# Starting the second mixture of experts inside linear attention, quantizing its successor's weights later, and three new orders around slot attention

## The chip, the cores and the metric

One core of one Trainium2 chip runs the whole network in a single launch. The metric is the device time in microseconds (us); the kernel before was run three times: 758.55, 759.08 and 763.17 us, median 759.08. Five engines work at the same time, each through its own list of instructions in order: TensorE (PE, matrix products into the accumulator memory PSUM), VectorE (DVE), ScalarE (ACT), GpSimd (POOL) and the queue SP that issues transfers. They are tied together by semaphores alone: an instruction waits until a counter has reached a number. Everything is 32-bit floating point.

## The reference, cut to what matters

The input is x, 8 batches of 512 tokens of 128 features. Six stages follow each other, each added to x (the layer norms have no weights):

```
x = x + 0.5 * MoE(layernorm(x))          # moe_a
x = x + LinearAttention(layernorm(x))    # linatt: causal, 16 heads of 8
x = x + 0.5 * MoE(layernorm(x))          # moe_b, same weights as moe_a
x = x + 0.5 * FFN(layernorm(x))          # ffn_a: fp4-quantized SwiGLU
x = x + SlotAttention(layernorm(x))      # att: softmax over the 8 batches, per token
x = x + 0.5 * FFN(layernorm(x))          # ffn_b, same weights as ffn_a

MoE: logits = xn @ router_w.T; top 2 of 8 experts, softmax over the two;
     expert: square(relu(xn @ w1[e])) @ w2[e]
FFN: q(xn) @ q(w_gate).T, q(xn) @ q(w_up).T; h = silu(gate) * up; q(h) @ q(w_down).T
q:   per block of 16: scale = max|.| / 6, round to {0, .5, 1, 1.5, 2, 3, 4, 6}, times scale
```

## The kernel before, in words

The program is one hand-written function. Inside it each engine has one list; per stage there is a function on each engine (`moe`, `linatt`, `ffn`, `att`), and the stages are called one after the other. The order of the calls in the code is the order on the engine; no planner exists. The whole x stays in on-chip memory (`x_sb`). A dictionary `S[stage]` holds the semaphores; `body(i, ...)` is the work of batch (or group, or slot) `i`, and early bodies stand in hardware loops (`Fori`).

**Mixture of experts.** For each of 8 batches (512 tokens) and 8 experts: TensorE makes `up(i, e)` (512 columns) into bank 2 or 3, ScalarE takes ReLU (L595) and then the square (L599), TensorE makes `down(i, e)` from the square (four products of 128x128) into one of the four banks 4 to 7, and VectorE adds it to x with the gate as factor (`accumulate`, L1070, four instructions). `down` waits until the bank was emptied four experts earlier (`out_free`). The gates come from `router` (TensorE), `gating` (VectorE, L1028 to L1047, ended by the ranks), an exponential `gate_exp` on ScalarE after expert 2 (L590), and `gating_end` (VectorE, L1051 to L1055). The layer norm of a later batch is statistics on VectorE (`ln_stats`, L985, L994), four small operations on GpSimd (`ln_group` or `layer_norm`), `normalise` on ScalarE (L577), `transposes` on TensorE and a copy back (`evac_xnT`, L584).

**Linear attention**, per batch: products, scores and states on TensorE; masks and the picking of head parts on VectorE (`scores` L1145, `pick` L1154 to L1165, `residual` L1173); `within` and `across` are the products inside and across chunks, in two halves; `project_out` is the last one. In its last batch only those steps are left. The weights of the feed-forward network lie in `fraw` (128x1152), and the object `w4` quantizes them on VectorE in these steps: `largest` L916, `scales` L922 and L924, `inverse` L935, `divide` L943, a magnitude on ScalarE (L533), `snap` L949, `unbias` L954, `rescale` L960. Before, the first five stand in the last batch of linear attention and the rest around the first gating of moe_b.

**Feed-forward**, per group of 512 tokens: quantize the normalised rows (`x_scales` on VectorE, `x_divide` on GpSimd, `x_squares` and `x_offsets` on ScalarE, `x_snap` on VectorE L1017, `x_back` on GpSimd L450 and L453, `x_transposes` on TensorE L1441, `evac_xnT`), four `gate_up(g, j)` (TensorE) with a `silu` each (ScalarE, L723), the product with the up-projection on VectorE (L1346; it opens the group), the quantization of the hidden values, transposes and `down`.

**Slot attention**, four slots of 1024 rows: VectorE makes query-key products (`qk`, L1239, eight), TensorE sums them per head (`score`), ScalarE copies (`scores_half`, L761), TensorE turns them (`turn`, L1710), VectorE subtracts the maximum (`less_max`, L1247), ScalarE takes exponentials, VectorE normalises and multiplies with the values (`pv`, L1267, eight), GpSimd adds pairs (`slot_pairs`, L408), TensorE sums (`context`, eight) and projects (`project_out`), ScalarE writes x (`x_out`, L773). The last slot also starts ffn_b.

## Time and profile before

| | us |
|---|---|
| median of three runs | 759.08 |
| the profiled execution, its own time | 757.82 |
| its span from first to last instruction | 756.0 |
| TensorE busy | 673.3 |
| VectorE busy | 606.9 |
| ScalarE busy | 458.5 |
| GpSimd busy | 294.7 |

Busy times overlap, so they do not add up to the span. A matmul's end is modelled in the profile. TensorE's granted clock over the whole span was 0.959 of full speed.

### The profile page before, as it was taken

What the parts mean: (1) busy time and instruction counts of PE and PEld (TensorE: products, weight loads), DVE (VectorE), ACT (ScalarE), POOL (GpSimd) and SP (SyncE); (2) the same over time, 40 slices, a digit from 0 to 9 for tenths busy, and PEclk for the clock granted to TensorE, in tenths of its full rate; (3) what the DMA queues carried; (4) which work ended last, traced back from release to release, by engine and by line L of the source; (5) the groups of instructions that cost most, each with busy time, mean ns of one, the idle gap of its engine ahead of it and who ended that gap; (6) DMA issues with size and microseconds to landing.
All of it is one profiled execution on the core that took longest, in us unless ns stands there. A gap on an engine that the chain in (4) does not pass through costs nothing.

```text
span 756.0 us, 16397 instructions
## 1 busy us (share of the span) xinstructions
PE 673.3 (89%) x5826; PEld 481.9 (64%) x5826; DVE 606.9 (80%) x1554; ACT 458.5 (61%) x867; POOL 294.7 (39%) x417
## 2 busy tenths in 40 slices
PE   4999999789999879999997789898978987799996
PEld 2777776567888757777764456565646556456664
DVE  2788787846766678887786999999999997899983
ACT  3787788674674328777786476757454433666642
POOL 5000120156556310011013677554534527668520
PEclk9999999879999989999999799999999998899996
DMA  8000000000000000000000000000000000000000
GB/s 207 22 0 0 0 1 1 0 3 4 2 0 3 4 1 1 0 0 0 0 1 2 0 1 0 1 2 0 3 0 0 0 0 1 0 29 15 24 19 29
DMA packets 13461, 7.08 MB, mean 9 GB/s; under 512 B 1177, under 2 KB 13409, under 8 KB 13409
## 3 DMA queue, kind: packets, MB, share of 16 engines
q1 hardware_dynamic: 11328, 5.33, 2.6%
q10 hardware_dynamic: 2080, 1.05, 0.5%
q8 instruction: 33, 0.54, 0.3%
q14 instruction: 20, 0.16, 0.1%
HBM read 4.28 MB, written 2.10 MB: 8 GB/s over the span
## 4 chain that ended last, share of the span: by engine, by line
PE 61%; DVE 18%; ACT 10%; issue 7%; POOL 3%; DMA 1%; DVEq 0%; POOLq 0%; ACTq 0%
PE ps L1427 56%; DVE shared L1267 4%; DVE shared L1239 3%; PE ps L1778 2%; DVE x_sb L1070 2%; ACT ffn_work L533 2%; ACT ffn_work L723 2%; PE ps L1435 1%; DVE stats L985 1%; ACT xnT L584 1%; ACT x_sb L832 1%; PE ps L1441 1%; ACT ffn_work L571 1%; ACT hqT L828 1%; DVE ps L1259 1%
## 5 line engine op out<-in xcount | busy, mean ns | idle before, releaser
L1427 PEld LDWEIGHTS ps<-w_sb,sq_h 128*128 128x128 f32 x1024 | 132.3, 193 | 70.6 <-ACT sq_h L599 51.8
L1070 DVE SCALAR_TENSOR_TENSOR x_sb<-ps,gates,x_sb 128x128 f32 (+1 forms) x512 | 147.2, 344 | 24.2 <-PE ps L1427 20.3
L1427 PE MATMUL ps<-w_sb,sq_h 128*128 128x128 f32 x1024 | 138.5, 279 | 1.8 <-ACT sq_h L599 1.8
L1427 PE MATMUL ps<-xnT,w_sb 128*128 128x512 f32 x256 | 135.7, 614 | 0.0
L353 POOL TENSOR_SCALAR vareps<-meanvar 128x4 f32<-128x4 f32 (+1 forms) x28 | 8.9, 319 | 265.7 <-DVE meanvar L994 265.3
L595 ACT ACTIVATE relu_h<-ps 128x512 f32<-128x512 f32 x128 | 75.6, 591 | 56.5 <-PE ps L1427 56.2
L599 ACT ACTIVATE sq_h<-relu_h 128x512 f32<-128x512 f32 x128 | 80.6, 630 | 4.0
L1427 PE MATMUL ps<-gateT,xnT 128*128 128x352 f32 x128 | 58.9, 544 | 14.7 <-ACT ffn_work L723 13.0
L577 ACT ACTIVATE xn<-x_sb,shift,rstd 128x128 f32 (+1 forms) x136 | 57.0, 481 | 10.1 <-POOL shift L361 8.3
L400 POOL TENSOR_TENSOR shared<-shared 128x128 f32<-128x128 f32 x112 | 51.0, 455 | 27.7 <-ACT shared L678 19.5
L1427 PE MATMUL ps<-downT,hqT 128*128 128x128 f32 x384 | 57.5, 289 | 4.2 <-ACT hqT L828 3.9
L1427 PEld LDWEIGHTS ps<-downT,hqT 128*128 128x128 f32 x384 | 49.4, 197 | 10.7 <-ACT hqT L828 10.4
L723 ACT ACTIVATE ffn_work<-ps 128x352 f32<-128x352 f32 x64 | 29.5, 461 | 40.3 <-PE ps L1427 40.2
L1427 PE MATMUL ps<-upT,xnT 128*128 128x352 f32 x128 | 51.5, 486 | 0.0
L828 ACT ACTIVATE hqT<-ps 128x384 f32<-128x384 f32 x64 | 29.6, 487 | 32.3 <-PE ps L1778 31.5
L408 POOL TENSOR_TENSOR shared<-shared 128x512 f32<-128x512 f32 x32 | 43.2, 1378 | 13.2 <-DVE shared L1267 13.2
L1427 PEld LDWEIGHTS ps<-gateT,xnT 128*128 128x128 f32 x128 | 21.3, 203 | 42.2 <-ACT ffn_work L723 33.3
L1239 DVE TENSOR_TENSOR shared<-shared 128x1024 f32<-128x1024 f32 x32 | 42.2, 1386 | 0.1
L1427 PEld LDWEIGHTS ps<-xnT,w_sb 128*128 128x128 f32 x256 | 40.1, 197 | 2.1 <-issue 2.1
L438 POOL TENSOR_TENSOR ffn_work<-xn,fq_x_r 128x512 f32<-128x512 f32 x16 | 16.9, 1057 | 59.3 <-DVE fq_x_r L939 59.3
L1427 PE MATMUL ps<-ident,shared 128*128 128x128 f32 x256 | 33.7, 287 | 6.1 <-POOL shared L408 6.0
L1346 DVE TENSOR_TENSOR ffn_work<-ffn_work,ps 128x1408 f32<-128x1408 f32 x16 | 25.9, 1619 | 15.9 <-PE ps L1427 15.9
(166 smaller groups left out, 1355.9 us busy)
## 6 DMA issues: line engine op xcount, KB each, us to landing
x_sb<-in_L_attn_x_dram SPq DMA_DIRECT2D x8, 256.0 KB, 7.5
out_dram<-x_sb SPq DMA_DIRECT2D x8, 256.0 KB, 2.3
w_sb<-in_L_ffn_w_all_dram ACTq DMA_DIRECT2D x2, 512.0 KB, 6.5
wraw<-in_L_attn_qkv_w_dram SPq DMA_DIRECT2D x1, 192.0 KB, 4.4
wraw<-attn_in_proj_weight_dram SPq DMA_DIRECT2D x1, 192.0 KB, 3.3
fraw<-in_L_ffn_w_down_dram SPq DMA_DIRECT2D x1, 176.0 KB, 3.1
fraw<-in_L_ffn_w_gate_dram SPq DMA_DIRECT2D x1, 128.0 KB, 2.7
fraw<-in_L_ffn_w_up_dram SPq DMA_DIRECT2D x1, 128.0 KB, 2.4
```

The source lines that it names most:

```text
L400: nc.gpsimd.tensor_tensor(st[:, k, :], st[:, k, :], st[:, k - 1, :], ALU.add).then_inc(s["prefix_ready"], 1)
L408: nc.gpsimd.tensor_tensor(prod[:, b, 0:B // 2, :], prod[:, b, 0:B // 2, :], prod[:, b, B // 2:B, :], ALU.add).then_inc(s["pair_ready"], 1)
L577: a = nc.scalar.activation(xn[:, into + j, :], tile(i, j), ACT.Identity, scale=rstd[:, j:j + 1], bias=shift[:, j:j + 1])
L595: nc.scalar.activation(relu_h[:, e % 2, :], bank(2 + e % 2, T), ACT.Relu).then_inc(s["relu_done"], 1)
L599: nc.scalar.activation(sq_h[:, e % 2, :], relu_h[:, e % 2, :], ACT.Square).then_inc(s["sq_ready"], 1)
L723: nc.scalar.activation(silu_g[:, j, :], bank(k, FI), ACT.Silu).then_inc(s["silu_ready"], 1)
L828: nc.scalar.activation(hqT[:, j % 2, :, :], bank(6 * (1 - j % 2), 3, P), ACT.Copy).then_inc(s["hT_ready"], 1)
L1070: t = nc.vector.scalar_tensor_tensor(tile_b(i, j), bank(4 + e % 4, TPB, C)[:, j, :], gates[:, j, e:e + 1], tile_b(i, j), ALU.mult, ALU.add)
L1239: nc.vector.tensor_tensor(prod[:, b, :, :], kT[:, :, :], qT[:, b, :].unsqueeze(1).to_broadcast([P, B, P]), ALU.mult).then_inc(s["qk_ready" ...
L1267: nc.vector.tensor_tensor(prod[:, b, :, :].rearrange("p a (h d) -> p a h d", h=H), v_att[:, :, :].rearrange("p a (h d) -> p a h d", h=H), ...
L1346: nc.vector.tensor_tensor(h3.rearrange("p (j k) w -> p j k w", k=KB), silu_g[:, :, :].rearrange("p j (k w) -> p j k w", w=BLK), ps[:, 2:6, ...
L1427: return nc.tensor.matmul(o, a, b, start=start, stop=stop, **kw)
```

## The change

Five things are changed, and no arithmetic is.

1. **moe_b begins inside the last batch of linear attention.** TensorE issues `router(0, 0)`, `up(0, 0)`, `up(0, 1)` and `down(0, 0)` between the steps of that batch; the first router writes bank 0 instead of bank 1 (`router_bank`). VectorE does `gating(0)` and `gating_end(0)` there, where the weights' quantization stood. The wait for all of linear attention (`x_done`) stands before the router of batch 1 now. Batches 0 and 1 are written out in front of the loops.
2. **The weights' quantization is spread**: `largest` and `scales` stay in linear attention (later in the batch), `inverse`, `divide` follow expert 1 of moe_b's batch 0, `snap` its expert 6, `unbias` and `rescale` experts 1 and 4 of batch 1. The magnitude on ScalarE follows expert 5 of batch 0.
3. **The last two batches of moe_b**: the statistics for ffn_a's first group stand after expert 4 of batch 6, not after expert 5.
4. **Slot attention's first half score** of a slot is issued at the end of the previous slot; that of slot 0 in the last group of ffn_a, in front of `down(7, 2)`, and its `turn` in front of the wait for ffn_a's results.
5. **Last slot and start of ffn_b**: `x_snap(0)` and `x_back(0)` earlier; `x_transposes` and `gate_up(0, 0)` after the second context, `gate_up(0, 1)` to `gate_up(0, 3)` in a row after the first `project_out`, and the last four contexts behind them.

```diff
@@ ScalarE, moe
-                        if e == 2:
+                        if e == 2 and (first or type(i) is not int or i > 0):
                             gate_exp(i)
+                        if e == 5 and not first and type(i) is int and i == 0:
+                            act.wait_ge(s_fv, 1)
+                            magnitude(fq_h[0][:, 0:6 * P + FK], fq_h[1][:, 0:6 * P + FK]).then_inc(s_fm, 1)
@@ ScalarE, last slot
                     exp_half(i, 1)
+                    evac_xnT(nxt, 0, k=2)
                     normal(nxt, False, 1)
+                    silu(nxt, 0, 0, 3)
                     ctx_half(i, 0)
                     x_out(i, 0)
-                    evac_xnT(nxt, 0, k=2)
-                    for j in range(TPB):
+                    for j in range(1, TPB):
                         silu(nxt, 0, j, 6)
-                    ctx_half(i, 1)
                     x_squares(nxt, 1)
                     x_offsets(nxt, 1)
+                    ctx_half(i, 1)
                     x_out(i, 1)
@@ VectorE, moe
-                        if e == 5 and more:
+                        if more and e == (5 if ahead or first else 4):
...
+                        if not first and type(i) is int and i < 2:
+                            if (i, e) == (0, 1):
+                                w4.inverse()
+                                w4.divide()
+                            if (i, e) == (0, 6):
+                                w4.snap()
+                            if (i, e) == (1, 1):
+                                w4.unbias()
+                            if (i, e) == (1, 4):
+                                w4.rescale()
@@ VectorE, last batch of linear attention
                     if not more:
-                        dve.wait_ge(s_fw, 80)
-                        w4.largest()
-                        w4.scales()
-                        w4.inverse()
+                        gating(0, lambda j: None)
                     pick(i, 0, side)
...
                     if not more:
-                        w4.divide()
+                        gating_end(0)
+                        dve.wait_ge(s_fw, 80)
+                        w4.largest()
+                        w4.scales()
                     pick(i, 1, side)
@@ VectorE, last slot
                     pv(i, 1)
+                    if not more:
+                        x_snap(nxt, 0)
                     less_max(i, 1)
...
                     pv(i, 3)
-                    if not more:
-                        x_snap(nxt, 0)
@@ TensorE, moe
+                    if not first and type(i) is int and i == 1:
+                        pe.wait_ge(S["linatt"]["x_done"], GROUPS)
...
-                    pe.wait_ge(s["out_free"], i * E + e + 1)
+                    if first or type(i) is not int or i > 0 or e >= 4:
+                        pe.wait_ge(s["out_free"], i * E + e + 1)
@@ TensorE, last slot
                     for b in range(4):
                         context(i, b)
+                        if not more and b == 1:
+                            pe.wait_ge(front.s["lin_ready"], 6 * TPB)
+                            x_transposes(nxt, 0, 2)
+                            gate_up(nxt, 0, 0, 3)
                     project_out(i, 0)
                     if not more:
-                        pe.wait_ge(front.s["lin_ready"], 6 * TPB)
-                        x_transposes(nxt, 0, 2)
+                        for j in range(1, TPB):
+                            if j > 1:
+                                pe.wait_ge(s["pv_ready"], B * i + 4 * (j - 1))
+                            gate_up(nxt, 0, j, 6)
                     for b in range(4, B):
                         context(i, b)
-                        if not more:
-                            if b >= 6:
-                                pe.wait_ge(s["pv_ready"], B * i + 4 * (b - 5))
-                            gate_up(nxt, 0, b - 4, 6)
                     project_out(i, 1)
+                    if more:
+                        front.score(i + 1, 0)
+                        front.turn(i + 1, 0)
@@ TensorE, ffn
                     hidden_transposes(g, 3)
+                    if first and g == GROUPS - 1:
+                        pe.wait_ge(s["hT_ready"], g * TPB + 3)
+                        front.score(0, 0)
                     down(g, 2)
```

On TensorE, in the last batch of linear attention and at the start of moe_b (`rT` is the router, `w1_sb` an up, `w2_sb` a down product, `wT,attT` a `project_out`, `shared` alone an `across`, `shared,v_tok` a `within`), the list before was:

```order
L1427 MATMUL ps<-shared,v_tok 32x128 x32
L1427 MATMUL ps<-shared 128x128 x7
L1427 MATMUL ps<-wT,attT 128x128 x4
L1427 MATMUL ps<-shared,v_tok 32x128 x32
L1427 MATMUL ps<-shared 128x128 x8
L1427 MATMUL ps<-wT,attT 128x128 x4
L1427 MATMUL ps<-rT,xnT 128x8 x4
L1427 MATMUL ps<-xnT,w1_sb 128x512
```

and now it is:

```order
L1453 MATMUL ps<-rT,xnT 128x8 x4
L1453 MATMUL ps<-shared,v_tok 32x128 x32
L1453 MATMUL ps<-shared 128x128 x7
L1453 MATMUL ps<-wT,attT 128x128 x4
L1453 MATMUL ps<-xnT,w1_sb 128x512
L1453 MATMUL ps<-shared,v_tok 32x128 x32
L1453 MATMUL ps<-shared 128x128 x8
L1453 MATMUL ps<-xnT,w1_sb 128x512
L1453 MATMUL ps<-w2_sb,sq_h 128x128 x4
L1453 MATMUL ps<-wT,attT 128x128 x4
```

The router, two up products and one down product now stand between the steps of linear attention.

On VectorE at the same place (`picked` and `attT` are a `pick`, `fq_h_max` is `largest`, the first row the last mask) the list before was:

```order
L1145 TENSOR_TENSOR shared<-ps,causal 128x512 x2
L916 TENSOR_REDUCE fq_h_max<-fraw 128x72
L922 TENSOR_SCALAR fq_h_s<-fq_h_max 128x72
L924 TENSOR_SCALAR fq_h_r<-fq_h_max 128x72
L935 RECIPROCAL fq_h_r<-fq_h_r 128x72
L1154 TENSOR_SCALAR picked<-ps,headsel 128x256
...
L1173 TENSOR_TENSOR x_sb<-ps,x_sb 128x512
L943 TENSOR_TENSOR ffn_work<-fraw,fq_h_r 128x1152
L1154 TENSOR_SCALAR picked<-ps,headsel 128x256
```

and now it is:

```order
L1170 TENSOR_TENSOR shared<-ps,causal 128x512 x2
L1038 COPY logits<-ps 128x32
L1041 TENSOR_REDUCE top<-logits 128x4
...
L1057 TENSOR_REDUCE rank<-diff 128x32
L1179 TENSOR_SCALAR picked<-ps,headsel 128x256
...
L1198 TENSOR_TENSOR x_sb<-ps,x_sb 128x512
L1061 SCALAR_TENSOR_TENSOR ex<-rank,exs 128x32
...
L926 TENSOR_REDUCE fq_h_max<-fraw 128x72
...
L1179 TENSOR_SCALAR picked<-ps,headsel 128x256
```

The gating took the place of the first four steps on the weights, and `gating_end`, `largest` and `scales` that of `divide`.

On TensorE in the last slot (`ident,shared` is a `context`, `wT,turned` a `project_out`, `ident,xn` the transposes for ffn_b, `gateT` and `upT` a `gate_up`) the list before was:

```order
L1427 MATMUL ps<-ident,shared 128x128 x16
L1427 MATMUL ps<-wT,turned 128x128 x4
L1441 MATMUL ps<-ident,xn 128x128 x4
L1427 MATMUL ps<-ident,shared 128x128 x4
L1427 MATMUL ps<-gateT,xnT 128x352
L1427 MATMUL ps<-upT,xnT 128x352
L1427 MATMUL ps<-ident,shared 128x128 x4
```

and now it is:

```order
L1453 MATMUL ps<-ident,shared 128x128 x8
L1467 MATMUL ps<-ident,xn 128x128 x4
L1453 MATMUL ps<-gateT,xnT 128x352
L1453 MATMUL ps<-upT,xnT 128x352
L1453 MATMUL ps<-ident,shared 128x128 x8
L1453 MATMUL ps<-wT,turned 128x128 x4
L1453 MATMUL ps<-gateT,xnT 128x352
L1453 MATMUL ps<-upT,xnT 128x352
```

Before, four pairs of `context` and `gate_up` followed the transposes; now one `gate_up` stands between the contexts, three follow `project_out` in a row, and four contexts (x16) come behind them.

## Rows read from the trace of the kernel before

**Rows 1.** The page: busy time, share and instructions of each engine; chain that ended last.

```profile
PE 673.3 (89%) x5826; PEld 481.9 (64%) x5826; DVE 606.9 (80%) x1554; ACT 458.5 (61%) x867; POOL 294.7 (39%) x417
...
PE 61%; DVE 18%; ACT 10%; issue 7%; POOL 3%; DMA 1%; DVEq 0%; POOLq 0%; ACTq 0%
```

**Rows 2.** Timeline, 261 to 284 us: start, us, engine, line, operation, [idle before <-releaser].

```profile
261.04 1.15 PE L1427 MATMUL ps<-shared,v_tok 32*32 32x128 f32 x64 [2.46 <-DVE shared L1145]
...
266.29 1.14 PE L1427 MATMUL ps<-shared,v_tok 32*32 32x128 f32 x64 [1.46 <-DVE attT L1165]
...
268.04 1.16 ACT L533 ACTIVATE ffn_work<-ffn_work 128x1152 f32<-128x1152 f32 x1 [15.01 <-DVE ffn_work L943]
...
271.67 1.16 PE L1427 MATMUL ps<-wT,attT 128*128 128x128 f32 x8 [2.26 <-DVE attT L1165]
...
275.11 1.36 DVE L954 SCALAR_TENSOR_TENSOR ffn_work<-ffn_work 128x1152 f32<-128x1152 f32 x1
...
281.39 1.05 PE L1427 MATMUL ps<-w_sb,sq_h 128*128 128x128 f32 x8
...
283.00 0.19 DVE L1051 SCALAR_TENSOR_TENSOR ex<-rank,exs 128x32 f32<-128x32 f32 x1 [2.93 <-ACT exs L590]
```

**Rows 3.** Windows: busy us of each engine, then TensorE's granted clock (PEclk).

```profile
276.00:280.00 4.00, 4.00 (x10) 1.93 (x9) 3.83 (x12) 2.05 (x4) 0.00 (x0) 0.50 0.00 0
...
630.00:640.00 10.00, 9.22 (x49) 8.09 (x49) 7.36 (x15) 3.98 (x6) 8.73 (x10) 0.73 0.01 2
```

**Rows 4.** Timeline, gating between batches 1 and 2 of moe_b.

```profile
310.12 0.35 DVE L1070 SCALAR_TENSOR_TENSOR x_sb<-ps,gates,x_sb 128x128 f32 x1 [1.15 <-PE ps L1427]
...
311.28 0.18 DVE L1038 TENSOR_TENSOR ex<-logits,top 128x32 f32<-128x32 f32 x1
...
313.81 0.21 ACT L590 ACTIVATE exs<-ex 128x32 f32<-128x32 f32 x1
```

**Rows 5.** Timeline, from batch 6 to batch 7 of moe_b.

```profile
388.01 0.88 ACT L577 ACTIVATE xn<-x_sb,shift,rstd 128x128 f32<-128x128 f32 x2 [1.80 <-POOL shift L429]
...
390.08 1.16 PE L1427 MATMUL ps<-w_sb,sq_h 128*128 128x128 f32 x8 [0.78 <-ACT sq_h L599]
...
393.55 0.19 DVE L1051 SCALAR_TENSOR_TENSOR ex<-rank,exs 128x32 f32<-128x32 f32 x1 [1.01 <-ACT exs L590]
```

**Rows 6.** Timeline, from ffn_a to the first slot.

```profile
517.36 10.37 DVE L1239 TENSOR_TENSOR shared<-shared 128x1024 f32<-128x1024 f32 x8
...
526.49 1.92 PE L1427 MATMUL ps<-shared,headcols 128*32 128x512 f32 x16 [1.26 <-ACT x_sb L832]
...
529.82 0.69 DVE L1247 TENSOR_REDUCE red<-ps 128x64 f32<-128x512 f32 x1 [2.09 <-PE ps L1710]
```

**Rows 7.** Timeline, last slot and the start of ffn_b.

```profile
621.19 0.69 DVE L1247 TENSOR_REDUCE red<-ps 128x64 f32<-128x512 f32 x1
...
625.92 1.65 DVE L1017 TENSOR_TENSOR ffn_work<-ffn_work 128x512 f32<-128x512 f32 x1
...
630.00 1.06 POOL L453 TENSOR_TENSOR xn<-ffn_work,fq_x_s 128x512 f32<-128x512 f32 x1
...
631.59 2.08 PE L1427 MATMUL ps<-wT,turned 128*128 128x128 f32 x8 [0.78 <-ACT turned L767]
...
635.73 0.76 PE L1427 MATMUL ps<-gateT,xnT 128*128 128x352 f32 x2
...
637.81 0.76 PE L1427 MATMUL ps<-gateT,xnT 128*128 128x352 f32 x2
...
643.35 1.62 DVE L1346 TENSOR_TENSOR ffn_work<-ffn_work,ps 128x1408 f32<-128x1408 f32 x1 [5.81 <-PE ps L1427]
...
645.13 0.60 ACT L773 ACTIVATE x_sb<-ps 128x512 f32<-128x512 f32 x1
...
649.79 1.51 PE L1427 MATMUL ps<-gateT,xnT 128*128 128x352 f32 x2 [0.73 <-issue]
...
658.03 1.62 DVE L1346 TENSOR_TENSOR ffn_work<-ffn_work,ps 128x1408 f32<-128x1408 f32 x1 [1.09 <-PE ps L1427]
```

More of the change, by code:

```diff
@@ L1128, in linatt @@
+                return gating, gating_end, run
+            def linatt(s, nxt, follow):
+                gating, gating_end, _ = follow
                 ch = Chain(dve, s["dve_chain"])
```

180 lines of the change are left out of this document (99 added, 81 removed).

## The prediction

> **What bounds the kernel now.** I read the page first, then the chain of waits and the timeline at the four places that the change touches. TensorE is busy for 89% of the span, VectorE for 80%; 61% of the chain that ended last is TensorE's, 18% VectorE's [rows 1]. So no one engine bounds the whole: the mixtures of experts run at TensorE's pace, slot attention and the feed-forward groups mostly at VectorE's. What the change can give lies where one stage hands over to the next, and there the rows show gaps. At the end of linear attention TensorE waits three times, 2.46, 1.46 and 2.26 us, each time for VectorE [rows 2]. Then moe_b starts from nothing: the second `down` product begins at 281.39, 9.7 us after the last `project_out` (271.67), and VectorE waits 2.93 us for the first exponential. From 276 to 280 TensorE's granted clock is 0.50, the 1.2 GHz level [rows 3]. Around batch 7 of moe_b ScalarE waits 1.80 us for a layer norm's shift [rows 5]. At the first slot VectorE waits 2.09 us [rows 6]; at ffn_b's start 5.81 us, and 1.09 us before its second group [rows 7]. These gaps together are the most that reordering can take out.
>
> **Part 1: moe_b begins early.** The router needs only batch 0's normalised rows, which were copied back long before; it goes in front of the `within` that begins at 261.04, inside a wait of 2.46 us. `up(0, 0)` goes in front of the one at 266.29, inside 1.46 us. `up(0, 1)` and `down(0, 0)`, about 1.8 us, go behind the last `across`, inside the 2.26 us before 271.67 [rows 2]. All four are hidden, and `project_out` keeps its place. VectorE's gating (some 2.3 us, as were the four steps on the weights that stood there) ends before `pick` can start. `gating_end`, `largest` and `scales` (about 2.6 us) replace `divide`, and fit in the 1.4 us of `divide` and the 1.5 us that VectorE waited there, with 0.1 us to spare. Up to 271.67 nothing moves. After it, `project_out` runs to 272.8, `up(0, 2)` takes 0.9, and `down(0, 1)` begins at about 273.6 in place of 281.39: **7.8 us** gained. Its square is ready, since ScalarE had nothing else to do.
>
> Against that: the magnitude (1.16 us, rows 2) used to run while ScalarE waited 15.01 us, and now stands behind expert 5, between squares for which TensorE waits. It costs between 0 (if the transposes cover it) and 1.16 us. I take 0.6, since transposes follow that expert. VectorE gets `inverse`, `divide`, `snap` (3.3 us) in batch 0 and `unbias`, `rescale` (2.7 us, two of 1.36, rows 2) in batch 1. The cover in batch 0 is that it begins to accumulate at once after the last residual: there is no wait of 2.93 us any more, and it has about 16 us for 17 us of work from a start that is earlier than TensorE needs. In batch 1 the 2.7 us make the next gating late. VectorE waits 1.15 us before that gating now, so 1.6 us remain; the difference that `gate_exp` needs is ready at 311.46 and used at 313.81 [rows 4], 2.35 us later. So 0.75 us of cover is left, and the banks that `down` needs come free over 2 us early. If the cover goes, what is late next is the exponential, and behind it on ScalarE every ReLU. I set this at 0. Part 1 is 7.8 - 0.6 = **7.2 us**. Bounds: 7.8 with the magnitude hidden; 3.8 if the clock falls to 1.2 GHz all the same for the 7 us that such a stretch lasts here (half of 7 is 3.4).
>
> **Part 2: statistics one expert earlier.** VectorE does them while it would wait for expert 5, so the shift that ScalarE waits for at 388.01 comes about 1.2 us earlier, of the 1.80 us. TensorE's wait of 0.78 us before 390.08 goes, and the exponential comes earlier, for which VectorE waits 1.01 us before 393.55; what VectorE does before it (`x_scales`) does not move [rows 5]. From there to ffn_a VectorE is busy with accumulations, so the end moves with it: **0.9 us**, between 0 and 1.0.
>
> **Part 3: half score 0 in ffn_a.** VectorE's fourth product ends half way through the eight that began at 517.36, at 522.6; the score (1.92 us) can run at 523.7, before two `down` products. Those, and the last `x_out` of ffn_a, are delayed by these 1.9 us, from 526.25 (the end of the wait before 526.49) to 528.2. The `turn` is done by then. `less_max` waits for that result too and starts at 528.2 in place of 529.82 [rows 6]: **1.6 us**, between 0 (if a table load falls between the copy and the exponential) and 2.1 (VectorE's whole wait). Queued behind the added wait on TensorE are only these `down` products. In the other slots the same instructions follow in the same sequence, and VectorE has no gap to give: 0.
>
> **Part 4: last slot and ffn_b.** `x_snap` moves from 625.92 to where `less_max` starts now, 621.19. The transposes wait for `x_back`, which ended at 631.06; 4.7 us earlier, and without a pair of GpSimd's in front of it, is 625.4. The pairs for contexts 2 and 3 now come behind `x_back` and a layer norm on GpSimd, and end at about 630, so `project_out` stays where it is (631.59). From its end three steps of `gate_up` and `silu` remain. A step with a context in it takes 2.08 us (635.73 to 637.81), without it between 1.2 (its own matmuls) and 2.08; I take 1.4, nearer to the matmuls. So the first group of ffn_b can start at about 637.5 to 638, which is also when VectorE is free (643.35 - 5.81 = 637.5): 5.6 us earlier [rows 7].
>
> Not all of it lasts. The four contexts that were mixed in now follow in a row (3.7 us), so the second `project_out` and its `x_out`, at 645.13 now, come only 1.5 to 2 us earlier. Behind that `x_out` on ScalarE stand the third layer norm and the copy for which `gate_up(1, 0)` at 649.79 waits. ScalarE no longer waits for GpSimd's `x_back(1)` between them, as that is early too, which gives 1.7 us more: `gate_up(1, 0)` at about 646.1. With the clock as now, the second group (658.03) moves by the same 3.7 us; from there the groups follow at their old distance. I take **3.7 us**. Upper end 5.3: the clock stays at 2.4 GHz here, and VectorE's own chain is the limit. Lower end 1.2: the clock falls before the first group as now (0.73 over 630 to 640, rows 3), and the contexts behind it are late.
>
> `x_snap` takes 1.65 us at 625.92, while GpSimd works on pairs. The Trainium skill ("SBUF — State Buffer", section "Who interferes with whom") says that a VectorE operation with two inputs in SBUF and a GpSimd operation that reads SBUF exclude each other, and the later one waits for the whole of the first. By that rule the new place, beside GpSimd's second pair, buys nothing in duration and the sum stays as below; without it the sum could grow by a part of these 1.65 us. I leave the duration at 1.65.
>
> **The sum.** 7.2 + 0.9 + 1.6 + 3.7 = 13.4 us. The profiled execution took 757.82 (span 756.0), so it would take 744.4. It lies 1.3 us under the median of the runs shown; from the median, 759.08 - 13.4 = **745.7 us**, which I name.
>
> **Rivals.**
> - *The clock falls in the last slot all the same.* For it: even now a fall lies there, and the new order still leaves gaps before the `gate_up`s. Against it: the longest gap, from the second context to the transposes, gets shorter and is filled by transposes and a `gate_up`. Part 4 then gives 1.2: 748.2 us. The Trainium skill ("TensorE: Matmul & The Clock Gate", section "A second HAM failure mode: psum-queue depth-cycling") says that short idle times between groups of matmuls can make the clock swing; it speaks for this rival. Chance 0.2.
> - *The clock falls at moe_b's start.* TensorE is denser from 261 to 273 than now, when it did fall [rows 2, 3]. Gain 3.4 less: 749.1 us. Chance 0.08.
> - *Slower: VectorE never catches up.* Place: gating in moe_b from batch 1 on. If each of the six later batches starts late by the 2.7 us of `unbias` and `rescale`, because TensorE's waits move along with VectorE and leave it no slack, that is 16.2 us lost against 13.4 gained: 761.9 us. It decides when the lateness passes the 2.35 us of cover [rows 4] and VectorE's waits are gone. Against it stands that VectorE waits 1.15 us in each batch now. Chance 0.03.
> - *The early start isn't early*: something that I take for ready (the exponential, the bank, `x_done`) holds moe_b back, and Part 1 shrinks to under 2 us: 751 us or more. Nothing in the rows speaks for it. Chance 0.07.
> - The forecast itself, 743 to 747: 0.57. The rest is a better case (both clocks high): 742.9.
>
> **How the numbers follow.** All upper ends: 7.8 + 1.0 + 2.1 + 5.3 = 16.2, so 742.9 from the median and 741.6 from the profiled execution. The low end is 741.5. The high end takes in both clock rivals together (745.7 + 2.5 + 3.4 = 751.6): 752. About 0.15 is left out. One per cent, 7.6 us, is what can be told from no change: under 751.5 is faster. Only the slower rival and part of the fourth lie above: faster 0.89, same 0.08, slower 0.03.
>
> **What would show it.** In the new profile: the router and `down(0, 0)` before the last `project_out`, and `down(0, 1)` at about 273.6; a granted clock of 1.00 from 273 to 281; no ScalarE wait before the normalise after batch 6; `less_max` 1.6 us earlier in its stage; the first group of ffn_b 5.6 us and the second 3.7 us earlier in their stage. Wrong would be: TensorE waiting for squares in batch 1 of moe_b, the exponential late, or a wait of some microseconds in front of the transposes in the last slot.

## The result and the profile after

| | before | after |
|---|---|---|
| first comparison, median (us) | 759.06 (4 runs, 758.55 to 763.17) | 740.63 (4 runs, 740.18 to 744.41) |
| all executions of this study, median | 758.58 (66 runs) | 741.27 (13 runs) |
| profiled execution, its own time | 757.82 | 744.41 |
| its span | 756.0 | 742.5 |
| granted clock over the span | 0.959 | 0.970 |

The ratio of the first comparison is 0.9759 (95% interval 0.9723 to 0.9796); of a second one, in five rounds, 0.9791 (0.9762 to 0.9821). The kernel is faster by 17 to 18 us where 13.4 were forecast: 740.63 lies 5.1 us under the 745.7 named, and just under the low end, 741.5. Between the two profiled executions the difference is 13.4 us, by chance the forecast to a tenth; two more profiled executions of the changed kernel took 742.32 and 741.70.

The page of the profile after, against [rows 1]:

```profile
PE 667.8 (90%) x5826; PEld 478.1 (64%) x5826; DVE 605.7 (82%) x1554; ACT 458.4 (62%) x867; POOL 295.1 (40%) x417
...
PE 64%; DVE 15%; ACT 10%; issue 6%; POOL 3%; DMA 1%; DVEq 0%; POOLq 0%; ACTq 0%
```

The same instructions, and the same busy times but for 5.5 us of TensorE and 1.2 of VectorE: waits and slow clock were taken out, not work, and the chain now runs through VectorE for 15% in place of 18%.

The timeline of the profile after, from linear attention's last batch to batch 2 of moe_b, against [rows 2, 4] (the lines of the code moved: L1453 was L1427, L536 L533, L593 L590, L1061 L1051):

```profile
260.07 1.06 PE L1453 MATMUL ps<-rT,xnT 128*128 128x8 f32 x8
...
262.60 1.96 PE L1453 MATMUL ps<-shared,v_tok 32*32 32x128 f32 x64 [1.48 <-DVE shared L1170]
...
267.96 0.48 DVE L1179 TENSOR_SCALAR picked<-ps,headsel 128x256 f32<-128x256 f32 x1 [3.31 <-PE ps L1453]
...
275.66 1.16 PE L1453 MATMUL ps<-wT,attT 128*128 128x128 f32 x8 [0.51 <-DVE attT L1190]
...
277.52 1.05 PE L1453 MATMUL ps<-w_sb,sq_h 128*128 128x128 f32 x8
...
284.46 1.15 ACT L536 ACTIVATE ffn_work<-ffn_work 128x1152 f32<-128x1152 f32 x1
...
294.42 0.21 ACT L593 ACTIVATE exs<-ex 128x32 f32<-128x32 f32 x1
...
309.95 0.21 ACT L593 ACTIVATE exs<-ex 128x32 f32<-128x32 f32 x1
...
310.28 0.19 DVE L1061 SCALAR_TENSOR_TENSOR ex<-rank,exs 128x32 f32<-128x32 f32 x1 [0.22 <-ACT exs L593]
```

The router fills a part of the wait (1.48 us remain of 2.46). `project_out` waits 0.51 us in place of 2.26, and the second `down` follows it after 1.86 us instead of 9.7. But the `within` at 262.60 took 1.96 us, not 1.15: the clock fell there, and VectorE waited 3.31 us. (The size of a clock fall is given below as what is missing to full clock: a stretch of 6.8 us at 0.50 is a fall of 3.4 us.) Windows of the same profile (granted clock third from the end):

```profile
262.00:270.00 8.00, 7.40 (x88) 6.48 (x88) 4.45 (x16) 0.23 (x1) 0.00 (x0) 0.57 0.01 3
273.00:281.00 8.00, 7.49 (x44) 5.40 (x43) 7.22 (x26) 3.95 (x7) 1.70 (x4) 1.00 0.00 0
628.00:636.00 8.00, 6.69 (x49) 5.76 (x48) 6.97 (x12) 3.20 (x7) 4.93 (x7) 1.00 0.01 2
636.00:640.00 4.00, 2.09 (x4) 1.18 (x4) 2.46 (x12) 3.54 (x7) 1.06 (x1) 0.72 0.00 0
```

The fall at 273 to 281 [rows 3] is gone, but one stands at 262 to 270. In the last slot the one over 630 to 640 is gone too, and a short one begins behind 637.

The rest of the timeline after, against [rows 5 to 7]: normalise and exponential of batch 7; half score and first maximum of slot 0; rounding step, GpSimd's pair, second maximum, and ffn_b's first two groups:

```profile
382.80 0.88 ACT L580 ACTIVATE xn<-x_sb,shift,rstd 128x128 f32<-128x128 f32 x2 [0.44 <-POOL shift L433]
...
388.41 0.21 ACT L593 ACTIVATE exs<-ex 128x32 f32<-128x32 f32 x1
...
517.74 1.92 PE L1453 MATMUL ps<-shared,headcols 128*32 128x512 f32 x16
...
522.07 0.69 DVE L1272 TENSOR_REDUCE red<-ps 128x64 f32<-128x512 f32 x1 [0.23 <-ACT x_sb L840]
...
613.45 0.85 DVE L1027 TENSOR_TENSOR ffn_work<-ffn_work 128x512 f32<-128x512 f32 x1
613.71 1.72 POOL L412 TENSOR_TENSOR shared<-shared 128x512 f32<-128x512 f32 x1
...
614.23 0.68 DVE L1272 TENSOR_REDUCE red<-ps 128x64 f32<-128x512 f32 x1
...
629.61 1.62 DVE L1371 TENSOR_TENSOR ffn_work<-ffn_work,ps 128x1408 f32<-128x1408 f32 x1 [0.78 <-PE ps L1453]
...
637.91 1.51 PE L1453 MATMUL ps<-gateT,xnT 128*128 128x352 f32 x2 [2.39 <-issue]
...
645.20 1.62 DVE L1371 TENSOR_TENSOR ffn_work<-ffn_work,ps 128x1408 f32<-128x1408 f32 x1 [0.37 <-PE ps L1453]
```

VectorE's waits of 2.09 us at slot 0, 5.81 and 1.09 us at ffn_b are down to 0.23, 0.78 and 0.37.

**Stage by stage.** A dozen instructions that occur in every version cut the span into stages: exponentials of moe_a (batch 7) and moe_b (batches 1, 6, 7), the product with the up-projection of ffn groups 0 and 1 (and 7), the maxima of the slots. Each number is the difference of two starts in a trace. The stages that are left out (batches 1 to 6 of moe_b, 77.96; groups 1 to 7, 75.86 to 75.90; slots 0 to 3, 84.57 to 84.83) differ in these eleven profiles by 0.26 us at most.

| profile | start to moe_a | linear attention, moe_b begins | batch 6 to 7 | to ffn_a group 1 | to slot 0 | slot 3 to ffn_b group 1 | end | span |
|---|---|---|---|---|---|---|---|---|
| before | 130.37 | 167.91 | 17.07 | 36.15 | 24.49 | 43.61 | 22.10 | 756.0 |
| before_look | 130.15 | 167.61 | 17.06 | 36.13 | 24.49 | 43.61 | 22.10 | 755.4 |
| after | 131.58 | 162.84 | 16.02 | 35.13 | 22.64 | 38.51 | 21.36 | 742.5 |
| after_again | 130.55 | 161.27 | 16.03 | 35.27 | 22.62 | 38.33 | 22.02 | 740.4 |
| after_look | 130.42 | 160.73 | 16.03 | 35.21 | 22.63 | 38.41 | 22.03 | 739.7 |
| part1_only | 130.47 | 163.08 | 17.06 | 35.92 | 24.49 | 42.46 | 22.14 | 750.2 |
| part2_only | 131.33 | 171.94 | 16.02 | 35.36 | 24.49 | 42.24 | 22.08 | 757.8 |
| part3_only | 130.73 | 168.73 | 17.06 | 35.76 | 22.62 | 42.03 | 22.02 | 753.3 |
| part4_only | 130.65 | 168.98 | 17.07 | 35.93 | 24.49 | 39.24 | 22.11 | 753.0 |
| snap_early_only | 130.20 | 168.13 | 17.06 | 35.76 | 24.50 | 43.70 | 22.03 | 755.7 |
| snap_late | 129.79 | 161.96 | 16.02 | 35.14 | 22.63 | 43.66 | 22.05 | 745.5 |

### The profile page after: what moved, and what is told of

It is laid out like the page before. It is cut to its first block, busy times and chain, and to the rows that moved or that the text cites. A ratio compares the mean times of both kernels' runs of the same rounds, so it can differ in the third digit from the quotient of the medians.

```text
span 742.5 us, 16304 instructions
## 1 busy us (share of the span) xinstructions
PE 667.8 (90%) x5826; PEld 478.1 (64%) x5826; DVE 605.7 (82%) x1554; ACT 458.4 (62%) x867; POOL 295.1 (40%) x417
## 3 DMA queue, kind: packets, MB, share of 16 engines
q10 hardware_dynamic: 2080, 1.05, 0.5%
## 4 chain that ended last, share of the span: by engine, by line
PE 64%; DVE 15%; ACT 10%; issue 6%; POOL 3%; DMA 1%; DVEq 0%; POOLq 0%; ACTq 0%
PE ps L1453 59%; DVE shared L1292 3%; DVE shared L1264 3%; PE ps L1826 2%; ACT ffn_work L731 2%; DVE x_sb L1081 2%; ACT ffn_work L536 2%; PE ps L1461 2%; ACT ffn_work L574 1%; ACT xnT L587 1%; ACT x_sb L840 1%; DVE stats L995 1%; PE ps L1467 1%; ACT ffn_work L569 1%; ACT hqT L836 1%
## 5 line engine op out<-in xcount | busy, mean ns | idle before, releaser
L1453 PEld LDWEIGHTS ps<-w_sb,sq_h 128*128 128x128 f32 x1024 | 132.1, 192 | 69.6 <-ACT sq_h L602 50.3
L1453 PE MATMUL ps<-w_sb,sq_h 128*128 128x128 f32 x1024 | 138.2, 278 | 1.4 <-ACT sq_h L602 1.3
L1453 PE MATMUL ps<-xnT,w_sb 128*128 128x512 f32 x256 | 134.3, 607 | 0.0
L1453 PE MATMUL ps<-gateT,xnT 128*128 128x352 f32 x128 | 57.4, 532 | 17.6 <-ACT ffn_work L731 13.4
L1453 PE MATMUL ps<-downT,hqT 128*128 128x128 f32 x384 | 57.0, 286 | 4.2 <-ACT hqT L836 4.0
L1453 PEld LDWEIGHTS ps<-downT,hqT 128*128 128x128 f32 x384 | 48.7, 195 | 11.6 <-ACT hqT L836 10.4
L1453 PEld LDWEIGHTS ps<-gateT,xnT 128*128 128x128 f32 x128 | 20.5, 198 | 46.4 <-ACT ffn_work L731 34.0
L1453 PE MATMUL ps<-upT,xnT 128*128 128x352 f32 x128 | 50.2, 475 | 0.0
L412 POOL TENSOR_TENSOR shared<-shared 128x512 f32<-128x512 f32 x32 | 43.3, 1380 | 13.1 <-DVE shared L1292 13.1
L1453 PEld LDWEIGHTS ps<-xnT,w_sb 128*128 128x128 f32 x256 | 39.7, 195 | 1.0 <-issue 1.0
L995 DVE BATCH_NORM_STATS2 stats<-x_sb 128x6 f32 (+1 forms) x144 | 30.7, 279 | 9.0 <-DMA x_sb<-in_L_attn_x_dram 5.1
L1292 DVE TENSOR_TENSOR shared<-shared,ps 128x1024 f32<-128x1024 f32 x32 | 37.2, 1215 | 0.6 <-DVE ps L1284 0.4
```

The lines of the kernel that those rows point to most:

```text
L412: nc.gpsimd.tensor_tensor(prod[:, b, 0:B // 2, :], prod[:, b, 0:B // 2, :], prod[:, b, B // 2:B, :], ALU.add).then_inc(s["pair_ready"], 1)
L995: ch.add(nc.vector.bn_stats(stats[:, j, :], tile(i, j)))
L1292: nc.vector.tensor_tensor(prod[:, b, :, :].rearrange("p a (h d) -> p a h d", h=H), v_att[:, :, :].rearrange("p a (h d) -> p a h d", h=H), ...
L1453: return nc.tensor.matmul(o, a, b, start=start, stop=stop, **kw)
```

## The experiments

Numbers after "measured" are the median, and the ratio to before with its 95% interval.

**The four parts alone.** Each is the kernel before with the lines of one part of the change and nothing else: part 4 (last slot and ffn_b), part 3 (half scores), part 1 (moe_b begun early, quantization spread), part 2 (one line). The lines are those of the diff further up:

```diff
-                        if e == 5 and more:
+                        if more and e == (5 if ahead or first else 4):
```

> Only the last slot and the start of ffn_b are in the new order. The prediction's size for it was 3.7 us (755.4). The trace of the change says more: between the last slots and ffn_b's second group it gained 5.1 us, and 0.7 at the end; by that theory this kernel takes 753.3, with the first group of ffn_b some 6 us and the second 5 us earlier in their stage, and one clock fall of 3.4 us less in 628 to 656. If the gain there needs the half score of part 3, it stays at 3.7 or under.

Measured: 755.05; 0.9944 (0.9922 to 0.9967). That is 3.5 us, by the median the prediction's 3.7 and not the 5.1 of the theory. In the profile the stage took 39.24 in place of 43.61, with the first group 5.3 and the second 4.4 us earlier, and one fall of 1.7 us stands in the last slot (629 to 632). That the gain needs part 3 is not so: further down the stage takes 38.86 without it.

> Only the half scores are moved: that of slot 0 into the last group of ffn_a, those of the other slots to the end of the slot before. The prediction said 1.6 us for slot 0 and 0 for the other slots (757.5); the trace of the change shows 1.85 at slot 0 (757.2). A rival: in the last slot, whose rest stays in the old order, the early score shifts TensorE's idle time and the clock, and the gain is 0 or 3.4 more.

Measured: 755.14; 0.9964 (0.9948 to 0.998). Slot 0's stage is 1.87 us shorter, as in the changed kernel; the other slots nothing. The last stage took 42.03 in place of 43.61. That is not the half score: part1_only and part2_only, which touch nothing there, took 42.46 and 42.24. In all three the first clock fall of the last slot is of 1.7 us, in before of 3.4. How long this stage takes in the old order depends on that fall.

> Only moe_b is begun early and the weights' quantization spread. The prediction said 7.2 us (751.9). Theory A: part 1 is worth 8 to 9 us where TensorE's clock does not fall inside linear attention's last batch, since the transition gains 7.8 and a clock fall less there gives more, so 750.5; the 5.1 us of the profiled execution of the change was a fall at 262 to 269. Theory B: that fall is there in most executions, and part 1 gives 5.1 us (754.0).

Measured: 749.76; 0.9881 (0.9862 to 0.99). Theory A by the timing (8.8 us, six executions), theory B by the stage (4.8 us, one execution, 163.08 for 167.91), as this profile has a fall of 3.4 us at 261 to 268.

> Only the statistics for ffn_a's first group are moved from expert 5 to expert 4 in moe_b's batch 6. The prediction said 0.9 us (758.2). The trace of the change shows 1.05 us at the exponential of batch 7, and 1.05 more before ffn_a's second group, where a VectorE wait for up-products shrinks from 1.00 to 0.37; if that belongs to this part, it is worth 2.1 us (757.0).

Measured: 758.51; 0.9994 (0.9975 to 1.0012). The two stages of this part are 1.05 and 0.4 to 0.8 us shorter in the profile, the median is not: its linear attention, which the change does not touch, took 171.94 with falls at 261 to 269 and 275 to 286. A microsecond of true gain drowns in that. Of part 2 only the stage is shown, not the time.

**Is the profiled execution typical?**

> The changed kernel once more, unaltered, for a second profiled execution. The first one's own time was 744.41, 3.8 above the median of its runs, with a fall of TensorE's clock at 262 to 270, inside linear attention's last batch. Theory A: in a usual execution that fall is absent or shorter, batch 1's exponential of moe_b stands some 3 us earlier than 294.42, and the median is 740.6. Theory B: the fall is there too, and the 3.8 us come from elsewhere (ffn_a's start, ffn_b, the beginning).

> The kernel before once more, for a second profiled execution. The first is 1.2 us under the median. Theory A: it was lucky at the end of linear attention (one clock fall, at 273 to 281, where four other profiles with the old order there have two), so from moe_a's last exponential to moe_b's second one this one takes 168.5 to 170 in place of 167.91. Theory B: that stage is the same and the difference lies in the last slot or the beginning.

> The changed kernel once more, a third profiled execution. Stage by stage the two profiles so far give 162.84 and 161.27 for linear attention and the start of moe_b. Theory A: the typical value is 161.3 to 162, the clock falls in linear attention's last batch in about half of the executions, and part 1 is worth 7 to 7.8 us. Theory B: it is nearer 160.5, and part 1 is worth the 8.8 us that it gained when timed alone.

Measured: after_again 741.58, 0.9791 (0.9762 to 0.9821); one execution each of the other two, 757.26 and 741.70. For before, neither theory: the second profile repeats the first in all stages within 0.3 us, and is 0.7 under the median of its comparison (757.98) again. For after, the first profile was the untypical one; the third has no fall in linear attention's last batch and takes 160.73 there, near the 160.5 of theory B. Windows of after_again:

```profile
262.00:270.00 8.00, 6.98 (x163) 5.82 (x164) 6.65 (x22) 1.46 (x3) 0.00 (x0) 1.00 0.02 5
...
273.00:281.00 8.00, 7.94 (x48) 5.92 (x49) 7.45 (x26) 5.30 (x11) 1.69 (x4) 1.00 0.00 0
```

and its timeline:

```profile
262.34 1.14 PE L1453 MATMUL ps<-shared,v_tok 32*32 32x128 f32 x64 [1.48 <-DVE shared L1170]
...
273.06 1.16 PE L1453 MATMUL ps<-wT,attT 128*128 128x128 f32 x8 [0.51 <-DVE attT L1190]
...
274.92 1.05 PE L1453 MATMUL ps<-w_sb,sq_h 128*128 128x128 f32 x8
...
291.82 0.21 ACT L593 ACTIVATE exs<-ex 128x32 f32<-128x32 f32 x1
```

No fall. From the last `within` to the second `down` it is 12.58 us, against 20.35 before [rows 2]: 7.77 us, where 7.8 were forecast. To batch 1's exponential it is 29.48, against 37.24 (261.04 to 298.28): 7.76, so the magnitude cost nothing on the way.

**Filling the wait in linear attention.** The changed kernel and behind the first router:

```diff
                         router(0, 0)
+                        pe.wait_ge(s["x_done"], GROUPS - 2)
+                        for _ in range(3):
+                            mm(bank(1, T), w1_sb[:, 0, :], xnT[:, 0:T])
                     within(i, 0, side)
```

> The changed kernel with three more products of 512 columns behind the first router, into bank 1, which nothing reads before it is overwritten; they fill TensorE's wait of 1.48 us before the last batch's within product. Theory A, the fall at 262 to 270 is set off by that wait: the granted clock stays at 1.00 there, and the median falls by up to 3 us, to 738 to 740. Theory B, it comes from the denser or sparser stretch before and is only moved: the same time within 1 us, a fall of 3.4 us elsewhere between 255 and 290. If the fillers are longer than the wait, up to 0.3 us is lost.

Measured: 742.44; 0.9793 (0.9767 to 0.9819). The three products took 2.82 us, more than the wait of 1.48 that they were to fill:

```profile
260.31 2.82 PE L1453 MATMUL ps<-xnT,w_sb 128*128 128x512 f32 x6
...
263.06 1.15 PE L1453 MATMUL ps<-shared,v_tok 32*32 32x128 f32 x64
```

No fall followed, but the time did not change. It tells little: after_again has none either, without a filler, and the filler is longer than the gap (the `within` begins 132.6 us after moe_a's last exponential, 131.8 in after_again). What sets the fall off stays open.

**Does VectorE catch up?** The changed kernel with the last step on the weights three times:

```diff
-                                w4.rescale()
+                                w4.rescale(2)
@@ def rescale(self, extra=0)
+                    for _ in range(extra):
+                        self.ch.need(self.ch.add(nc.vector.tensor_tensor(self.dst3, blocks(self.v), self.wide(self.sl), ALU.mult)))
```

> The changed kernel with the rescaling of the weights done three times instead of once, in batch 1 of moe_b after expert 4: 2.7 us more for VectorE just before the gating of batch 2. In the trace of the change that gating's end waited 0.22 us for the exponential. The prediction's slower rival said that a lateness there repeats in each of the six later batches (up to 15 us more). The forecast said that it is a single delay, caught up through VectorE's waits of about 1.15 us a batch: exp(2) up to 2.5 us later, and 0 to 2.5 us in all.

Measured: 746.28; 0.9845 (0.9816 to 0.9875). Its exponential of batch 2 waited for VectorE:

```profile
302.14 2.74 DVE L971 TENSOR_TENSOR fraw<-ffn_work,fq_h_s 128x1152 f32<-128x1152 f32 x2
...
310.98 0.23 ACT L593 ACTIVATE exs<-ex 128x32 f32<-128x32 f32 x1 [1.45 <-DVE ex L1050]
```

Of 2.72 us added (two operations of 1.36), 1.55 were lost at batch 2 (exponential to exponential 17.08 in place of 15.53) and 1.2 covered. The four later batches together lost 0.05. It is a single delay, and the rival's mechanism is refuted. The rest of the 5.0 us over 741.27 goes in part with TensorE's clock. Linear attention's stage is 2.1 us longer than in after_again, with a fall of 3.4 us at 261 to 268 that the latter has not. Another at 609 to 616 cost nothing that its stage shows (38.41).

**The magnitude elsewhere.** The changed kernel with

```diff
-                        if e == 5 and not first and type(i) is int and i == 0:
+                        if e == 3 and not first and type(i) is int and i == 0:
```

> The changed kernel with the magnitude on ScalarE behind expert 3 of moe_b's batch 0, where a half of a layer norm's rows follows it (0.86 us) and no transposes, in place of behind expert 5. The prediction set its cost behind expert 5 at 0.6 us because transposes cover it; the traces show 0 there (from the second down product to batch 1's exponential 16.90 us, 16.89 before). If the transposes are the cover, down products are late by up to 1.16 us here and stay so; if ScalarE's free half microsecond per expert is the cover, nothing is lost (within 0.3 us) by batch 1's exponential.

Measured: 746.0; 0.982 (0.9801 to 0.9839).

```profile
281.37 1.16 ACT L536 ACTIVATE ffn_work<-ffn_work 128x1152 f32<-128x1152 f32 x1 [1.34 <-DVE ffn_work L953]
...
284.50 0.84 PE L1453 MATMUL ps<-w_sb,sq_h 128*128 128x128 f32 x4 [2.26 <-ACT sq_h L602]
```

More than either theory said: ScalarE waits 1.34 us for VectorE's `divide`, then spends 1.16, TensorE waits 2.26 us, and a clock fall of 1.7 us follows. From the second `down` (276.82) to the exponential (297.72) it is 20.90 in place of 16.90. An operation that is free at expert 5 costs 4 at expert 3. The input's readiness decides, which neither theory had named; which of the two covers it is at expert 5 was not separated.

**The halves of part 4.** The changed kernel with VectorE's `x_snap` in its old place (snap_late), and the kernel before with only `x_snap` on VectorE and `x_back` on GpSimd early (snap_early_only):

```diff
@@ snap_late, VectorE, last slot
-                    if not more:
-                        x_snap(nxt, 0)
                     less_max(i, 1)
...
                     pv(i, 3)
+                    if not more:
+                        x_snap(nxt, 0)
```

> The changed kernel with VectorE's rounding step for ffn_b's first group back in its old place, after the fourth value product of the last slot; TensorE's and ScalarE's new order stays. If the early rounding is what part 4 lives on, ffn_b's first group starts 4 to 5 us later relative to its slot (22.92 us after the slot's first maximum now) and the second 3 us later, so the kernel takes about 743.5; if TensorE's order is what counts, the loss is under 1 us. The rounding took 0.85 us in the new place and 1.65 in the old one; here it should take 1.65 again.

> The kernel before with one half of part 4 alone: VectorE's rounding step and GpSimd's step back for ffn_b's first group early, the order of TensorE and ScalarE as before. With the other half alone (the kernel with the late rounding) the second group of ffn_b stood 43.7 us after the third slot's maximum, with both 38.5, in the old order 42.0 to 43.6. If the early rounding works by itself, about 39 to 40 is seen here; if the two halves only work together, 42 to 43 and a time equal to before's. My estimate is 41: the transposes still stand behind the first project_out, which moves by nothing.

Measured: snap_late 746.44, 0.9843 (0.9813 to 0.9873); snap_early_only 759.27, 1.0011 (0.9992 to 1.003). As cut here, each half gives nothing: 43.66 and 43.70 us for the stage, 43.61 with neither in before (42.0 to 42.5 in the three profiles named above), 38.4 with both. The expected 41 and 743.5 were missed. The rounding step early is of no use while the transposes stand behind `project_out`, and the transposes early wait for the rounding step (VectorE then waits 6.10 us):

```profile
615.45 0.69 DVE L1027 TENSOR_TENSOR ffn_work<-ffn_work 128x512 f32<-128x512 f32 x1
...
616.22 1.26 POOL L454 TENSOR_TENSOR ffn_work<-ffn_work 128x512 f32<-128x512 f32 x1 [3.96 <-DVE ffn_work L1027]
...
631.98 1.62 DVE L1371 TENSOR_TENSOR ffn_work<-ffn_work,ps 128x1408 f32<-128x1408 f32 x1 [6.10 <-PE ps L1453]
```

The step took 0.69 us here, not the 1.65 expected; no pair of GpSimd's runs beside it.

snap_late is not the new order of TensorE and ScalarE alone. GpSimd's `x_back` stays in its new place, in front of two pairs, and waits there 3.96 us for the late rounding step. The pairs behind it then begin 16.6 us after the slot's first maximum (11.3 in before, 13.1 in the changed kernel), and the first `project_out` 22.7 us after it (17.2 and 17.6). In snap_early_only `x_back` stands in front of the same two pairs, and `project_out` begins at 18.7. So the step and `x_back` belong together; the new order of TensorE and ScalarE with GpSimd's old order was not timed.

**Two tries to gain more** at ffn_b's start, on top of the changed kernel; the second adds one product in the wait of 2.39 us before `gate_up(1, 0)`:

```diff
@@ ScalarE, ffn_b: copy of the second group's rows first
-                normal(s, first, 2)
                 evac_xnT(s, 1)
+                normal(s, first, 2)
@@ VectorE, ffn_b, group 0
+                    dve.wait_ge(s["rstd_ready"], 3)
+                    moments(3)
                     x_scales(s, ch, g + 2)
@@ TensorE (ffnb_filled only), behind x_transposes(s, 1)
+                    pe.wait_ge(s["silu_ready"], TPB)
+                    mm(bank(6, TPB, C), ident[:, :], out_b_all[:, :].unsqueeze(1).to_broadcast([P, TPB, C]))
```

> A try to gain more. The changed kernel with two steps at ffn_b's start in another order: ScalarE copies the second group's transposed rows before it normalises the third group's, and VectorE does the fourth group's statistics (1.2 us) before the third group's maximum, for which it waited 1.51 us. The up products of the second group then come up to 1.1 us earlier and VectorE's waits shrink; the second product with the up-projection should stand 0.6 to 0.9 us earlier than 15.5 us after the first. Against it: TensorE runs at 1.2 GHz for 1.7 to 3.4 us there, and if those products are late VectorE waits for them instead, and nothing is won.

> The same, and one product of 512 columns into an unread bank in TensorE's wait of 2.39 us between the second group's transposes and its gate products, behind which the granted clock falls in all runs so far. Theory A, the idle time sets the fall off: the clock stays at 1.00, the second group's products take 1.4 in place of 2.4 us each and the group starts another 0.4 us earlier. Theory B: the fall comes all the same and nothing changes against the kernel without the filler.

Measured: 742.48, 0.9801 (0.9778 to 0.9825); and 741.58, 0.9781 (0.9759 to 0.9803). The first group to the second is 15.34 and 15.35 us in place of 15.44 to 15.59, and groups 1 to 7 are 0.2 longer. The fall behind 636 was absent in both, with and without the filler, so it is not the filler. Nothing is won, and there is no version that beats the changed kernel.

**Do the parts add up?** The changed kernel without the lines of part 2, and without those of part 3:

> The changed kernel without part 2, the statistics of ffn_a's first group back behind expert 5. Alone, part 2 moved the time by nothing that five rounds could tell, while its own two stages were 1.05 and 0.65 us shorter in the profiles. If parts simply add up, this takes 1 to 1.7 us more than the changed kernel (741.1 over its two sets of runs), so 742.5; if part 2 only shows in the whole, up to 3 us more (744).

> The changed kernel without part 3, each half score back at its slot's start. Alone, part 3 took 3.4 us off the median, of which the profile shows 1.86 at slot 0 and nothing in the other slots. If its worth is the 1.86 of that stage, this takes 743.0; if it is worth 3.4 in the whole too, 744.5, and then a stage other than slot 0 must be longer, most likely the last slot, where the score now stands in front.

Measured: 743.58, 0.98 (0.977 to 0.9831); and 745.09, 0.9827 (0.9796 to 0.9857). Against 741.27 they cost 2.3 and 3.8 us. In the profiles, part 2 missing is 1.03 at batch 7 (17.06), 0.5 to ffn_a's group 1 (35.70) and 0.6 in the last slot's stage (39.05); part 3 missing is 1.89 at slot 0 (24.52) and 0.45 in the last slot (38.86), the latter each time with a clock fall of 1.7 us at 617 to 623 that the whole change has not. Alone the parts took 8.8, 0, 3.4 and 3.5 us off the median, 15.7 together, and the whole 17.3: they add up within what these medians can tell. Against the forecast's 7.2, 0.9, 1.6 and 3.7 these medians put the surplus on parts 1 and 3, not on part 4 (see below).

## Why the prediction was wrong

The direction held, and so did the mechanism of each part but for TensorE's clock in part 4; the size was too small, 13.4 for 17.3 us (medians of all executions). The means of two profiles of each kernel (before and before_look, after_again and after_look) give each term:

| term | forecast | measured, by its stage |
|---|---|---|
| part 1 | 7.2 | 6.8 (167.76 to 161.00) |
| part 2, batch 7 | 0.9 | 1.0 |
| part 2, ffn_a's start | not named | 0.9 (36.14 to 35.24) |
| part 3 | 1.6 | 1.9 |
| part 4 | 3.7 | 5.2 (43.61 to 38.37) |
| sum | 13.4 | 15.8 |

- **The term that was mis-sized is part 4**, at the step "With the clock as now, the second group (658.03) moves by the same 3.7 us". Measured are 5.2, the upper end (5.3) that I had given for a clock that stays up. The first group came 6.0 us earlier in its stage (forecast 5.6) and `gate_up(1, 0)` 4.2 (forecast 3.7); from there to VectorE's next product it is 7.1 to 7.3 us in place of 8.25. In before the last slot and ffn_b's start hold two falls of 3.4 us each (629 to 635, 649 to 656); in the changed kernel there is one of 1.7. The first of the two lies on the first `project_out`: the 2.08 us of [rows 7], which the forecast carried along, are 1.16 in the changed kernel. A fall is a part of the gap that one removes, and the gap was priced without it.
- **How far that is shown.** Against part1_only, part2_only and part3_only, where the first fall is half as large and `project_out` takes 1.16 us, the stage is 3.6 to 4.1 us shorter, which is the forecast; against before and before_look, from whose rows the forecast was worked out, it is 5.2. So the 1.5 us between go with the clock. This rests on comparing profiles; no run changed the clock and nothing else. And the medians of the parts alone (8.8, 0, 3.4 and 3.5 us) do not single out part 4.
- **The rival that the clock falls in the last slot all the same** (chance 0.2) did not come in the three profiles of the whole change. In part4_only, all_but_part2 and all_but_part3 such a fall of 1.7 us is there; the stage takes 38.9 to 39.2, so it costs 0.5 to 0.9 us, not the 2.5 that I gave it. In vector_burdened and ffnb_order one stands at the slot's very start and costs nothing (38.41 and 38.27).
- **Part 1** is right in its mechanism to 0.03 us (7.77 for 7.8 at the second `down`). The magnitude, 0.6, costs 0. About 1 us goes the other way before the last batch's `within`, in a part that the change leaves alone: TensorE waits for nothing that the profile shows (marked issue: 0.48 us at 256 in before, 1.03 in after_again, but 0.49 in after_look), and the batches before take 0.6 to 0.7 longer; why was not found. Of the twelve profiles of kernels with part 1, eight show a clock fall of 1.7 to 3.4 us (missing to full clock) at 261 to 270, which adds to the scatter: the stage takes 160.5 to 162.1 us without one, 161.3 to 162.0 with 1.7, 162.8 to 163.3 with 3.4 (magnitude_at_3 aside). Of the six without part 1, four show one too, beside that at 273 to 286, which none with part 1 has (that of magnitude_at_3, at 285, follows its own wait). So part 1 took out the fall at moe_b's start and shows no sign of making the earlier one. "Up to 271.67 nothing moves" holds for the waits, not for the clock. The rival of a fall at moe_b's start did not come.
- **VectorE's cover** in batch 1 of moe_b: forecast 0.75 us left after the 2.7; measured 1.2, by the burdened kernel. No ReLU and no square was late.
- **Part 2**: the shift's wait went from 1.80 to 0.44 (I had expected none), TensorE's 0.78 us to 0, the exponential 1.05 earlier. Behind it another 0.9 came at ffn_a's start, where I had only said that the end moves along. It is there in nine of the eleven profiles with part 2 (35.09 to 35.36, in the seven without it 35.70 to 36.15), but magnitude_at_3 and ffnb_order took 36.28 with part 2. So the 0.9 is not sure, and its cause was not settled: the clock falls of that start sum to 6.8 us in before and in after_again alike.
- **Part 3**: 1.9, inside its bounds. The score stands where it was put, the `down` products and the last `x_out` behind it are delayed as forecast, and of VectorE's wait of 2.09 us 0.23 are left, for that `x_out`.
- **The last step, from the profile to the median.** I took the sum from the profiled execution and subtracted it from the median, which was 1.3 us higher, as if that distance belonged to any version. The two executions of the changed kernel in the table (742.32, 741.70) stand 0.4 to 1 us above their median, those of before 0.8 to 1.3 below. That makes 1.8 of the 3.9 us; 2.4 are the table's, and the other stages take 0.3 back. It may be chance: 66 executions of before reach from 754.98 to 763.46, 13 of the changed kernel from 739.74 to 745.76. Within one kernel the time goes with the granted clock, which is on record for each execution (part2_only: four between 754.89 and 755.93 at 0.965, eight between 757.9 and 760.27 at 0.954 to 0.959). But the clock does not explain this distance: both profiled executions of before have 0.959, as most of the slower ones do. So it stays open.
- The slower rival (VectorE never catches up) is refuted, and that the early start isn't early too.

The rounding step: I left its duration at 1.65, because beside GpSimd's pair the new place should buy nothing. It took 0.85. The Trainium skill ("SBUF — State Buffer", section "Who interferes with whom") says that the later of two such operations waits for the whole of the first. The trace agrees to 0.15 us: the step began 0.3 us before the first pair ended, lost about 0.16 us against the 0.69 of snap_late, and the pair behind it took 1.72 in place of 1.27; in the old place it began 0.17 us behind the start of a pair and lost 0.96. The rule was right and my use of it wrong: what it costs is the rest of the other's operation, and that depends on the place. The other place of the Trainium skill that I named ("TensorE: Matmul & The Clock Gate", section "A second HAM failure mode: psum-queue depth-cycling") says that short idle times between groups of matmuls can make the clock swing, and spoke for a fall in the last slot. The three profiles of the whole change show none there before 636, part4_only, all_but_part2 and all_but_part3 show one.

## What to carry to other kernels

When a reordering closes a gap, count with the gap what the slow clock behind it costs now, and give that its own term: here it went with the difference between 3.7 and 5.2 us. Two moves can be worth nothing each and four to five microseconds together (43.7, 43.7, 38.4 us), so undo them one at a time and both at once before either is called useless, and look at what else waits for the one that is undone. And profile a kernel more than once before its sum is taken to a tenth: one execution's stages outside the change differed by 1 to 4 us.

## What had not been expected of the hardware

- A piece of one engine's work can be free at one place and cost over three times its own length at another (magnitude: 0 us behind expert 5, 4.0 us behind expert 3), because a wait for its input is added and a clock fall of 1.7 us follows on TensorE.
- Clock falls repeat in some executions and move in others. before and before_look both show nine, with 31.3 us missing to full clock inside the span; after_again and after_look five at the same places, with 19.5 us; but the first profile of the same changed kernel shows eight, with 22.2.
- A clock fall need not cost time. The fall of 1.7 us at 588 to 591 in before cost nothing: slots 0 to 3 took 84.60 us, and 84.57 in after_again, which has none there. One of 3.4 us in linear attention's last batch goes with 2 us.
